# A graph kernel's attention stage: the order of the work on TensorE, VectorE and ScalarE, and a first radial layer over all 128 rows

## The reference

```python
# layer 0, graph attention, 4 heads of 64 channels, self loops included
h = x @ W
e = leaky_relu(a_src[src] + a_dst[dst], 0.2)
alpha = exp(e - segment_max(e, dst)[dst])
agg = segment_sum(h[src] * alpha, dst) / segment_sum(alpha, dst)
x = layernorm(x + elu(agg + bias + x @ skip_W))
# layer 1, equivariant convolution; a radial network gives each edge 256 weights
h = silu(edge_attr_8 @ fc_w1 / sqrt(8))
h = silu(h @ fc_w2 / sqrt(64))
w = h @ fc_w3 / sqrt(64)
msg = products of w, of the edge's 4 numbers and of node features at dst
out = normalise(segment_sum(msg, src) @ w2 + x @ wsc)
x = layernorm(x + out)
```

## Time and profile before

| what | value |
|---|---|
| median of 3 runs | 6377.99 us (6374.91 to 6380.39) |
| span of the profiled execution | 6385.1 us |
| the profiled execution's span against the median | 7.1 us more |
| attention stage in the profile, about | 180 to 2310 us |
| message stage of layer 1, about | 2760 to 6080 us |

### The profile page before, as it was taken

How to read it: one execution, slowest core, us unless ns; L and a number is a source line. 1 busy time by engine, 2 the same in 40 slices (tenths; PEclk the granted TensorE clock), 3 DMA queues, 4 the chain that set the end, 5 groups by cost and what they waited for, 6 DMA issues and landing times.

```text
span 6385.1 us, 227589 instructions
## 1 busy us (share of the span) xinstructions
PE 5967.2 (93%) x48182; PEld 4370.4 (68%) x48183; DVE 5501.1 (86%) x17614; ACT 3747.7 (59%) x12831; POOL 4714.7 (74%) x4057
## 2 busy tenths in 40 slices
PE   6899999999999988899999999999999999999976
PEld 5555555555555555567777777777777777777754
DVE  2899999999999989988888888888888888888878
ACT  2566666666666654456666666666666666666622
POOL 2777777777777755557777777777777777777778
PEclk8999999999999988899999999999999999999999
DMA  5889998888898864479999999999999999999998
GB/s 192 227 263 263 263 264 263 263 263 264 264 264 263 263 206 152 154 149 165 166 166 165 166 165 166 166 166 165 166 166 165 166 166 166 166 166 166 165 284 293
DMA packets 1269305, 1298.01 MB, mean 203 GB/s; under 512 B 220815, under 2 KB 1180560, under 8 KB 1269168
## 3 DMA queue, kind: packets, MB, share of 16 engines
q0 software_dynamic: 328176, 468.28, 46.5%
q1 hardware_dynamic: 941090, 829.29, 42.2%
HBM read 695.18 MB, written 601.74 MB: 203 GB/s over the span
## 4 chain that ended last, share of the span: by engine, by line
PE 54%; issue 3%; DVE 3%; POOL 2%; DMA 0%; ACT 0%; DVEq 0%; POOLq 0%; SPq 0%; ACTq 0%
PE PS L973 12%; PE PS L952 11%; PE PS L941 11%; PE PS L989 9%; PE PS L1003 6%; PE PS L1000 2%; PE PS L911 1%; POOL d_n L603 1%; DVE arena L1274 1%; PE PS L961 1%; DVE arena L1266 1%; POOL out L597 0%; DVE stat L1282 0%; PE PS L919 0%; PE PS L960 0%
## 5 line engine op out<-in xcount | busy, mean ns | idle before, releaser
L585 POOL DMA_INDIRECT part<-arena,c_idx x1664 | 2585.6, 1554 | 759.1 <-issue 708.2
L546 POOL DMA_INDIRECT big<-h_tab,big x1664 | 1632.0, 981 | 512.0 <-PE PS L864 244.6
L864 PE MATMUL PS<-big 128*128 128x260 f32 x3328 | 952.9, 409 | 162.5 <-DVE big L1171 156.9
L660 ACT ACTIVATE big<-PS,arena 128x128 f32<-128x128 f32 x1664 | 513.6, 359 | 667.0 <-PE PS L854 667.0
L1179 DVE TENSOR_TENSOR big<-big,PS 128x260 f32 x1664 | 699.8, 421 | 210.1 <-PE PS L864 152.8
L952 PE MATMUL PS<-arena 128*128 128x256 f32 x3328 | 869.2, 384 | 1.6 <-DVE arena L1340 1.3
L973 PE MATMUL PS<-arena,w2m 64*64 64x128 f32 (+2 forms) x13312 | 859.2, 316 | 0.0
L864 PEld LDWEIGHTS PS<-big 128*128 128x128 f32 x3328 | 563.8, 189 | 422.1 <-issue 227.0
L1316 DVE TENSOR_TENSOR arena<-PS,arena 128x384 f32<-128x384 f32 x832 | 463.7, 557 | 426.3 <-PE PS L989 413.7
L941 PE MATMUL PS<-ident,arena 128*128 128x128 f32 x4992 | 728.6, 282 | 1.2 <-DVE arena L1350 1.2
L730 ACT COPY arena<-PS 128x384 f32<-128x384 f32 x1664 | 722.0, 491 | 3.2 <-PE PS L941 3.2
(11 more groups left out here) (182 smaller groups left out, 11630.3 us busy)
## 6 DMA issues: line engine op xcount, KB each, us to landing
w_tab<-big SPq DMA_DIRECT2D x416, 520.0 KB
arena<-w_tab SPq DMA_DIRECT2D x1664, 130.0 KB
part<-arena SPq DMA_DIRECT2D x1664, 32.1 KB
ot_tab<-big SPq DMA_DIRECT2D x416, 128.0 KB
arena<-ot_tab SPq DMA_DIRECT2D x416, 128.0 KB
arena<-src_tab SPq DMA_DIRECT2D x416, 128.0 KB
arena<-part SPq DMA_DIRECT2D x392, 128.5 KB, 3.5
big<-h_tab,big POOLq DMA_INDIRECT x1664
```

Source lines behind the costliest of these rows:

```text
L546: pool.indirect_dma_start(hg[:, s, k, :], None, h_tab, bass.IndirectOffsetOnAxis(ap=sidx[:, s, k:k + 1], axis=0)).then_inc(s_hg[s], 16)
L585: pool.indirect_dma_start(part[q], bass.IndirectOffsetOnAxis(ap=c_idx[:, s, k:k + 1], axis=0), o_cmb[:, s, k, :], None, compute_op=ALU.add ...
L864: mm(PS[:, 2 + k % 2, 0:HW], oh[:, p, k, :], hg[:, p, k, :], start=True, stop=True).then_inc(s_agg, 1)
```

## The change

In `step_a` of TensorE the third layer moves ahead of all four sums, and the second layer stands between sums 1 and sums 2, where it stood behind sums 3. In VectorE's, the second `half_silu` (h2) and all four messages come first, and the four additions follow with the small logit instructions and the first `half_silu` (h1) between them. In ScalarE's, both pairs of `radial_weights` and both tanh come before the exponent. The first radial layer multiplies by all 128 rows of `fc1` and of `eat` (rows 16 to 127 are zero), not by 16.

```diff
-        fc1 = cut(P)[0:2 * NBAS, :]
+        fc1 = cut(P)
@@ ScalarE
                     radial_weights(0)
-                if there(g - 1):
-                    wait(act, s_z, 5 * g)
-                    a.activation(hg[:, m, :, D:HW], za[:, m % 2, :, :], ACT.Exp).then_inc(s_p, 1)
-                if there(g - 3):
                     radial_weights(1)
-                if there(g + 3):
-                    sources(g + 3, (s + 3) % TURN)
@@ ScalarE, behind the two tanh
+                if there(g - 1):
+                    wait(act, s_z, 5 * g)
+                    a.activation(hg[:, m, :, D:HW], za[:, m % 2, :, :], ACT.Exp).then_inc(s_p, 1)
+                if there(g + 3):
+                    sources(g + 3, (s + 3) % TURN)
@@ TensorE
+                if there(g - 3):
+                    third_layer()
                 if there(g - 2):
                     sums(0)
                     sums(1)
-                if there(g - 3):
-                    third_layer()
                 if there(g):
                     b = numbers(pe, block_row, g * GROUP, GROUP, NB)
-                if there(g - 2):
-                    sums(2)
-                    sums(3)
                 if there(g - 1):
                     wait(pe, s_h1, g)
                     wait(pe, s_h2, g - 1)
                     mm(PS[:, 7, 0:2 * P], fc2[:, :], h1[:, m % 2, :], start=True, stop=True).then_inc(s_f2, 1)
+                if there(g - 2):
+                    sums(2)
+                    sums(3)
                 if there(g + 1):
                     wait(pe, s_ea[n], landed(g + 1, n))
                     wait(pe, s_h1, g + 1)
-                    mm(PS[:, 6, 0:2 * P], fc1[:, :], eat[0:2 * NBAS, n, :], start=True, stop=True).then_inc(s_f1, 1)
+                    mm(PS[:, 6, 0:2 * P], fc1[:, :], eat[:, n, :], start=True, stop=True).then_inc(s_f1, 1)
@@ VectorE, prologue
+            v.memset(eat[:, :, :], 0.0)
@@ VectorE
                 if there(g - 2):
+                    wait(dve, s_t2, g - 1)
+                    wait(dve, s_f3, 2 * (g - 3))
+                    half_silu(h2[:, o % 2, :], t2[:, o % 2, :], PS[:, 7, 0:2 * P]).then_inc(s_h2, 1)
                     wait(dve, s_p, g - 1)
                     message(0)
                     message(1)
                     message(2)
+                    message(3)
```

More of the change, by code:

```diff
@@ L1192, in step_a @@
                                     AX.X, ALU.add).then_inc(s_z, 1)
[L1193 to L1196, removed]
+                if there(g - 2):
+                    add_up(0)
                 if there(g - 1):
@@ L1201, in step_a @@
                 if there(g - 2):
-                    add_up(0)
+                    add_up(1)
                 if there(g - 1):
@@ L1205, in step_a @@
                     leaky(zb[:, m % 2, :, :], za[:, m % 2, :, :]).then_inc(s_z, 1)
+                if there(g):
+                    wait(dve, s_t1, g + 1)
+                    wait(dve, s_f2, g - 1)
+                    half_silu(h1[:, s % 2, :], t1[:, s % 2, :], PS[:, 6, 0:2 * P]).then_inc(s_h1, 1)
                 if there(g - 2):
-                    message(3)
+                    add_up(2)
                 if there(g - 1):
@@ L1212, in step_a @@
                 if there(g - 2):
[L1213 to L1217, removed]
+                    add_up(3)
                 if there(g - 1):
@@ L1221, in step_a @@
                     v.tensor_scalar(za[:, m % 2, :, :], za[:, m % 2, :, :], 0.0, None, ALU.min).then_inc(s_z, 1)
-                if there(g - 2):
-                    add_up(3)
                 if there(g + 2):
```

## The result

| | median us | runs from | to |
|---|---|---|---|
| before | 6379.19 (4 runs) | 6374.91 | 6385.85 |
| changed | 6410.12 (4 runs) | 6406.37 | 6411.01 |

The ratio is 1.0044, with a 95% interval of 1.003 to 1.0058, which is 28 us (19 to 37). The medians differ by 31 us; the forecast was 22 us more than before, 6400 us. The profiled execution of the changed kernel took 6409.49 us, with a span of 6407.6.

The account below looks back on a forecast made before the run. The TensorE/VectorE loop, 5.13 us a group, would fall to 4.94, below GpSimd's 5.01; adding 0.18 stretch gives 5.19, 0.05 to 0.06 above 5.13, times 416: +22 us with the fill, 6400 us, range 6336 to 6440.

Parts of the forecast that it names:

- GpSimd's floor at 5.00: Attention stage: four gathers of 0.95 us, each with a 0.30 us gap, take at least 5.00 us a group.
- The loop of TensorE and VectorE at 5.13: Kernel before: sums, third layer, addition 3, L1226 and message 0 form a loop that sets the pace, 5.13 us a group.
- What stretches a gather: A gather waits, 0.13 us behind its start, for an already running VectorE instruction reading two SBUF operands, ending 0.82 us later.
- VectorE's round of 4.94: Changed kernel: VectorE's work of 4.47 us, 0.22 lost twice between additions, and sums 0.03 late make 4.94 us a group.
- The rival with a round of 5.01 to 5.10: VectorE's round is a little longer than added up, so it sets the pace: -50 to -13 us, chance 0.25.
- POOL then sets the pace, with a stretch of 0.18: Changed kernel: gathers pace the group at 5.01 us plus 0.18 taken by VectorE's two-input instructions, 5.19 us.
- the working's mean over all phases: Average stretch of four gathers by messages and L1226 over all phases: 0.21 us a group.
- VectorE waits at L1200 for each group's last gather to land: Changed kernel: the landing fixes VectorE's phase; as a sign, L1201 waits for the h_tab DMA in most groups.
- PE's wait for messages: Sign that the forecast is right: TensorE's wait for messages grows beyond 0.37 us.
- The fixed phases of the working: Landings 2.75, 3.1 or 3.47 us behind the last gather's end stretch a group by 0.11, 0.46 or 0.17 us.
- The covered parts: First layer on TensorE (0.44 us a pair), moved third and second layers, and ScalarE's later exponent all fit in spare time.
- The Trainium skill's rule: VectorE instructions with two SBUF inputs and GpSimd's SBUF reads lock a shared port pair for the whole instruction; forecast followed rows instead.

Follow-up runs that it names:

- the kernels with 8 and 12 blocks: Changed kernel, VectorE's L1193 summing 8 or 12 column blocks instead of 4, extras unread: 6341.52 us (0.9932) and 6373.66 us (0.9981); on the slow chip 7230.33 and 7234.97.
- the variant with three gathers: Fourth tile's rows fetched by SyncE, not gathered: changed kernel 6500.56 us (1.018), kernel before 6487.61 (1.0161); on the slow chip 6896.71 (0.9717) and 6838.68 (0.9638).

## Why the prediction was right

**What bounds the kernel now.** GpSimd's floor at 5.00: borne out. The lowest group time measured, 5.04, stands just above it, and the mean of 0.955 us there is within 0.005 of the undisturbed gather of the earlier trace rows. The loop of TensorE and VectorE at 5.13: likely, but no run tested it, since the one that was to do so brought SyncE's bound. What speaks for it are the waits of the kernel before, one each way in every group, and none of VectorE for a landing in the same 1200 us:

```profile
PE PS L864 <- DVE big L1171: 87.6, 234, 0.4
DVE big L1179 <- PE PS L864: 85.8, 233, 0.4
```

One link of the working's loop is wrong: VectorE waits for sums 2 at addition 2 (1004.19), and addition 3 follows 0.65 behind because it waits for addition 2, not for the end of sums 3. That the sum left nothing over is no support: differences along one timeline always close.

**What stretches a gather**: borne out. Followed over all 1664 gathers of each of the eight kernels with four gathers a group on the usual chips, it gives the length to within 30 ns in 98.6% to 99.9% of them.

**VectorE's round of 4.94**: right in the sum. From L1225 to L1225, 964.08 to 969.25 and 969.25 to 974.37, it takes 5.17 and 5.12 us here, waits included; in 600 to 1800 us the shortest round is 4.90 and a quarter are under 4.96. Two runs put its turning point to the test. With 0.10 more it came to 5.04, with 0.20 more to 5.11, so the unhindered round is 4.91 to 4.94. The rival with a round of 5.01 to 5.10 (chance 0.25, -50 to -13 us) thus describes the kernels with 8 and 12 blocks, at -44 and -11 us, the second just past its end.

**POOL then sets the pace, with a stretch of 0.18**: the mechanism holds, and the size was 0.20 (5.21 less 5.01). The difference of 0.02 is 8 us, and the forecast was 9 us short. The term is one of phase, and it was a choice between 0.11 and 0.46; that it fell so near is in part luck. Counted over the gathers of 600 to 1800 us, messages stretch a group by 0.12 and the one-hot instruction by 0.08, where the working's mean over all phases gave about 0.10 to each.

**"VectorE waits at L1200 for each group's last gather to land"**: too strong. It waits 87 times in 231 groups, so the sign "in most groups" failed. A second sign failed too: **PE's wait for messages**, which was to grow beyond 0.37, is gone. The third layer now stands ahead of the sums and ends about when message 0 does. In its place TensorE waits 100 times in 231 groups, 50.7 us in all, and always at sums 3 for addition 1. The working had looked at sums 2 and addition 0 alone ("0.03 late"), and took additions 0 and 1 to be 0.65 apart: where L1201 waits for a landing, addition 1 stands behind it, and sums 3 and all after it are late by as much. Additions 2 and 3 are 0.65 apart, additions 0 and 1 from 0.65 to over 1.0. So VectorE loses the time in some groups and not in others, and the phase wanders: where it waits, L1201 starts 2.6 to 5.1 us behind the last gather's end, with a median of 3.3. The fixed phases of the working (2.75, 3.1, 3.47 us) are points of that walk, and their mean over all phases, 0.21, was the better estimate. The working's picture of one phase for all groups is thus the step that was wrong, and it cost little here.

**The covered parts**: the first layer took 968.94 - 968.51 = 0.43 us a pair from start to start, as the 0.44 said, and undoing it alone moved nothing. The exponent brought no named wait before a message in 600 to 1800 us. Moving the third layer was costed as covered, and in the whole change it is; alone it costs 121 us. That the second layer, which takes its place between sums 1 and 2, makes the difference is argued: the changed kernel has another order on VectorE as well, and no run moved the second layer alone.

**The Trainium skill's rule** on the exclusive lock ("SBUF — State Buffer", section "SBUF: two separate sides") names the right partners. Its length, the whole instruction, does not fit here either: in the timeline after, a gather of 1.18 us and four messages of 1.43 us run together from 965.08 on, and the gather waits for the end of message 0 alone.

## What to carry to other kernels

- An engine at 74% over the span can be the next bound of one stage: divide the stage by its instructions there, and look whether busy time and fixed gaps together fill it. The gain from speeding the others ends at that sum.
- When two engines with nearly equal rounds can hold each other up, the faster one's spare time is spent in the collision. The best place here was a round just above the other's floor, and it is worth trying a little more work as well as a little less.
- Before moving an instruction, ask what wait it was filling. It may be needed there more than the instruction that waits for it.

## What was not expected of the hardware

- In every kernel with four gathers a group on the usual chips, each gather of 600 to 1800 us has a gap of 0.303 to 0.317 us before it, whatever releases it.
- A wait of a gather for a VectorE instruction is not made good, and it can be long. In the kernel with the third layer alone moved, a gather that starts 0.12 us after L1226 takes 0.43 more than the next:

```profile
1000.77 1.38 POOL L546 DMA_INDIRECT big<-h_tab,big  x1 [0.31 <-issue]
1002.46 0.95 POOL L546 DMA_INDIRECT big<-h_tab,big  x1 [0.31 <-issue]
```

- The same kernel before took 6379 to 6385 us in four sessions and 7099 us in a fifth, on a chip of its own. It was not traced there, but the kernel with 8 blocks was on both, and the attention stage took its extra time: 7.10 us a group against 5.04, times 416, is 857 of the 889 us between its two runs. On it the variant with three gathers was 3% faster, and the one with 8 blocks 2% slower: a change tuned on one chip can turn its sign on the other.
